# DLRM tower with two CIN layers: moments tiled by class, contraction at each chunk's end, dense layers per chunk

## What is computed

```python
e = stack([tbl_f[ids[:, f]] for f in range(32)], axis=1)        # (512, 32, 64)
x1 = einsum('oc,bcd->bod', W0, outer(e, e)) + b0                # outer: (512, 32*32, 64)
x2 = einsum('oc,bcd->bod', W1, outer(e, x1)) + b1               # outer: (512, 32*128, 64)
z = concatenate([x1.sum(2), x2.sum(2)], axis=1)                 # (512, 256)
h = relu(concatenate([z, dense_ctx], 1) @ W_top1 + b_top1)      # (512, 512)
y = relu(h @ W_top2 + b_top2) @ W_top3                          # (512, 1)
```

## Time and profile before

| | |
|---|---|
| median of 3 runs | 286.87 us |
| the profiled execution, its own time | 285.69 us |
| its span, first to last instruction | 283.9 us |
| TensorE busy (matmul records) | 244.8 us |
| TensorE loading weights | 177.0 us |
| ScalarE busy | 162.9 us |
| GpSimd busy (all but 0.6 of it gathers) | 143.2 us |
| VectorE busy | 132.7 us |

### The profile page before, as it was taken

How to read it: one execution, slowest core, us unless ns; L and a number is a source line. 1 busy time by engine, 2 the same in 40 slices (tenths; PEclk the granted TensorE clock), 3 DMA queues, 4 the chain that set the end, 5 groups by cost and what they waited for, 6 DMA issues and landing times.

```text
span 283.9 us, 6021 instructions
## 1 busy us (share of the span) xinstructions
PE 244.8 (86%) x2356; PEld 177.0 (62%) x2356; DVE 132.7 (47%) x350; ACT 162.9 (57%) x471; POOL 143.2 (50%) x134
## 2 busy tenths in 40 slices
PE   0699981149778997999999999999999999999985
PEld 0588870125545545777768777879777779995331
DVE  0100399355778928865607765626766620000111
ACT  0488883035566996669875668886566664001100
POOL 5777789777777777777777777700000000000000
PEclk9999998557999999999999999999999999999999
DMA  4911100011111112421111431100230000351000
GB/s 138 346 37 25 30 15 9 19 24 30 23 23 29 22 29 61 110 58 20 30 25 24 122 79 22 29 7 0 60 95 0 2 2 0 93 161 52 0 0 0
DMA packets 10366, 13.14 MB, mean 46 GB/s; under 512 B 4161, under 2 KB 5313, under 8 KB 10338
## 3 DMA queue, kind: packets, MB, share of 16 engines
q1 hardware_dynamic: 5058, 8.23, 9.7%
q0 software_dynamic: 4096, 4.20, 7.7%
q10 hardware_dynamic: 1184, 0.32, 0.6%
HBM read 8.54 MB, written 0.00 MB: 30 GB/s over the span
## 4 chain that ended last, share of the span: by engine, by line
PE 59%; POOL 26%; issue 10%; DMA 3%; DVE 1%; SPq 0%; ACT 0%; POOLq 0%
POOL XG L231 26%; PE psum L530 18%; PE psum L458 11%; PE psum L507 9%; PE psum L518 6%; PE psum L548 3%; PE psum L592 3%; PE psum L535 3%; DMA main<-in_w1t 3%; PE psum L486 2%; PE psum L586 2%; PE psum L588 1%; PE psum L520 1%; PE psum L587 1%; DMA XG<-in_tbl,idx 1%
## 5 line engine op out<-in xcount | busy, mean ns | idle before, releaser
L231 POOL DMA_INDIRECT XG<-in_tbl,idx x128 | 142.6, 1114 | 40.9 <-issue 38.1
L349 ACT ACTIVATE main<-psum 128x256 f32<-128x256 f32 (+5 forms) x324 | 104.7, 372 | 38.1 <-PE psum L520 16.5
L311 DVE TENSOR_TENSOR PP<-main 128x512 f32<-128x512 f32 x128 | 82.8, 689 | 31.4 <-PE psum L507 31.3
L530 PEld LDWEIGHTS psum<-main,DT 128*128 128x128 f32 x512 | 64.4, 191 | 24.9 <-issue 24.4
L530 PE MATMUL psum<-main,DT 128*128 128x128 f32 x512 | 77.4, 285 | 0.0
L349 ACT ACTIVATE U<-psum 128x512 f32<-128x512 f32 (+1 forms) x129 | 49.6, 436 | 31.5 <-PE psum L507 25.4
L507 PE MATMUL psum<-PP,main 64*32 64x320 f32 x1024 | 50.2, 450 | 4.9 <-DVE PP L317 4.9
L518 PE MATMUL psum<-ident,U 128*128 128x128 f32 x256 | 38.8, 274 | 1.2 <-ACT U L349 0.9
L518 PEld LDWEIGHTS psum<-ident,U 128*128 128x128 f32 x256 | 29.6, 141 | 6.9 <-issue 3.9
L486 PE MATMUL psum<-ident,XG 128*128 128x128 f32 x128 | 20.8, 291 | 14.4 <-DMA XG<-in_tbl,idx 12.4
L275 DVE TENSOR_TENSOR main<-main 128x240 f32<-128x240 f32 (+15 forms) x62 | 18.9, 382 | 17.3 <-ACT main L349 17.3
(11 more groups left out here) (45 smaller groups left out, 114.4 us busy)
## 6 DMA issues: line engine op xcount, KB each, us to landing
main<-in_w1t SPq DMA_DIRECT2D x4, 512.0 KB, 8.8
XG<-in_tbl,idx POOLq DMA_INDIRECT x128, 2.7
GL<-main SPq DMA_DIRECT2D x32, 64.0 KB
GG<-main SPq DMA_DIRECT2D x32, 64.0 KB
main<-in_wt SPq DMA_DIRECT2D x2, 512.0 KB, 4.1
W0Z<-in_w0z SPq DMA_DIRECT2D x1, 512.0 KB, 11.2
GG<-in_near_a ACTq DMA_DIRECT2D x1, 136.0 KB, 2.4
GG<-in_near_b ACTq DMA_DIRECT2D x1, 136.0 KB, 2.7
```

Of the source, the lines that this page charges most:

```text
L231: pool.indirect_dma_start(out=XG[:, f, :], out_offset=None, in_=tables[f], in_offset=bass.IndirectOffsetOnAxis(ap=idx[:, c, f:f + 1], axis=0),
L311: v.tensor_tensor(pp[:, :, g * P:(g + 1) * P].rearrange("p b (s j) -> p b s j", s=NS), in_main(at, [[2 * XW, KB], [0, NS], [1, HF]]), in_m ...
L349: return a.activation(dst, src, ACT.Copy)
L530: mm(z, DT[:, m, t, :], T[:, (c + 1) % 2, t].rearrange("p (h m) b -> p h m b", h=2)[:, :, m, :], start=m == 0 and t == 0, stop=False)
```

## The change

- The moments are tiled by class: the 256 near pairs, the small class and x itself form 16 blocks of 20 columns, 320 in all, cut into four classes of 80. Class q goes into the array's column tile q, for each sample: a step has 32 matmuls of 80 columns, into the same two banks. ScalarE copies 640 elements per partition straight into U, which holds a whole chunk; `turn`, T, T2 and the DMAs on SP go away.
- Products are made for 8 samples per half at a time (j counts them, 8 per chunk, two steps each) with two buffers PP. The columns with x itself are written by ScalarE (`e_columns`).
- The contraction of a chunk (8 + 69 matmuls of 128 columns) stands after its last step, all in one piece, with the x groups 4 to 7 of the next chunk in it, after 8, 28, 51 and 77 matmuls. Groups 0 to 3 stand behind j = 0, 2, 4 and 6.
- The dense layers of chunk c run with 128 columns inside chunk c+1, those of the last chunk at the end. Their weights are loaded at the start.
- The coefficient matmuls come in another order (near and cross by halves of the fields), nine of the 18 coefficient groups are transposed ahead of x group 7 of chunk 0, the others two per j in chunk 0, copied by ScalarE.
- A gather of chunk c, fields f to f+7, waits for NG*c + f//4 - 2 transposed groups. In chunk 0 gathers from field 12 on wait for coefficient matmuls.

The diff, cut to its core:

```diff
+NBK = 2 * NS
+BW = HF + 4
+NP = NBK * BW
+NQ = 4
+CW = NP // NQ
+TB = HF + 1
+NT = NBK // NQ * TB
+NN = NT + 1
 BP = P // 2
 KB = 4
 NK = BP // KB
-CL = 2 * P
-CX = CL + F
-NP = CX + F
+NJ = NK // 2
+KP = 2 * KB
 XW = HF + NS
-PPS = 3
+PPS = 2
 F1, F2 = 512, 256
 DC = 16
-NQ = 4
 NG = 8
-XK = 7
-NDT = F // 2 + 2
+NDT = (NN + 3) // 4
+NE = 9
+VORDER = [*[("near", m) for m in range(HF)], *[("cross", m) for m in range(HF, F)],
+          *[("near", m) for m in range(HF, F)], *[("cross", m) for m in range(HF)]]
+
+XPAIR = {0: 0, 2: 1, 4: 2, 6: 3}
+TURN = ((8, 4), (20, 5), (23, 6), (26, 7))
...
+def coefficient_groups(j):
+
+    return range(NE + 2 * j, min(NE + 2 * j + 2, NDT))
...
+    uses = [("x", 0, g) for g in range(NG - 1)] + [("d", 0, n) for n in range(NE)] + [("x", 0, NG - 1)]
...
-            by = pair_dve if use[0] == "d" and use[2] % 3 != 1 else pair_act
+            by = pair_dve if use[0] == "d" and use[2] % 2 and use[2] < NE else pair_act
...
             sp.dma_start(idx[:, :, :], ids).then_inc(ids_in, 16)
-            sp.dma_start(CROSS, cross_a).then_inc(cross_in, 16)
-            sp.dma_start(CROSS_B, cross_b).then_inc(cross_in, 16)
             for i in range(4):
                 sp.dma_start(W1T[:, 8 * i:8 * i + 8, :], w1t[:, 8 * i:8 * i + 8, :]).then_inc(w1_in[i], 16)
+                if i == 1:
+                    sp.dma_start(CROSS, cross_a).then_inc(cross_in, 16)
+                    sp.dma_start(CROSS_B, cross_b).then_inc(cross_in, 16)
             sp.dma_start(W0Z[:, :, :], w0z).then_inc(w0z_in, 16)
-            for c in range(NC):
-                sp.wait_ge(b7_ev, use7["t2", c, NK - 1] + 1)
-                if c:
-                    sp.wait_ge(z0_mm, c)
-                else:
-                    sp.wait_ge(dt_mm, NDT)
-                for q in range(4):
-                    for h in range(2):
-                        for dst, r in ((GL, 0), (GG, F)):
-                            sp.dma_start(
-                                dst[32 * q:32 * q + 32, h, :, :],
-                                T2[64 * h + r:64 * h + r + F, c % 2, 8 * q:8 * q + 8, :],
-                            ).then_inc(g_in, 16)
-                if c == NC - 1:
-
-                    sp.dma_start(WT1, wt1[0:2 * P, :].rearrange("(k p) n -> p k n", p=P)).then_inc(mlp_in, 16)
-                    sp.dma_start(WT1C, wt1[2 * P:, :]).then_inc(mlp_in, 16)
-                    sp.dma_start(WT2, wt2.rearrange("(k p) n -> p k n", p=P)).then_inc(mlp_in, 16)
+            sp.dma_start(WT1[:, :, :], wt1[0:2 * P, :].rearrange("(k p) n -> p k n", p=P)).then_inc(mlp_in, 16)
+            sp.dma_start(WT1C[:, :], wt1[2 * P:, :]).then_inc(mlp_in, 16)
+            sp.dma_start(WT2[:, :, :], wt2.rearrange("(k p) n -> p k n", p=P)).then_inc(mlp_in, 16)
...
                 for f in range(F):
                     if c and f % 8 == 0:
                         pool.wait_ge(gathered[f // 8], 128 * c)
-                    if c and f % 4 == 0:
-                        pool.wait_ge(x_mm, NG * (c - 1) + f // 4 + 1)
+                    if c == 0 and f % 4 == 0 and f >= 12:
+                        pool.wait_ge(v_mm, 2 * (f - 8))
+                    if c and f % 8 == 0:
+                        pool.wait_ge(x_mm, NG * c + f // 4 - 2)
...
+            dve.wait_ge(v_ev, F)
+            for _ in moves(1):
+                pass
+            wrap_field(0)
+            dve.wait_ge(v_ev, 2 * F)
+            for _ in moves(0):
+                pass
+            for n in range(NE):
+                coefficients_out(n)
...
-            def products(c, k):
-
-                n = NK * c + k
+            def products(c, j):
+
+                n = NJ * c + j
                 if n >= PPS:
-                    dve.wait_ge(t_mm, n - PPS + 1)
-                pp = PP[:, n % PPS]
-                x0 = (c % 2) * xt_n + KB * k * 2 * XW + NS
+                    dve.wait_ge(t_mm, 2 * (n - PPS + 1))
+                pp = PP[:, n % PPS].rearrange("p b (s w) -> p b s w", w=BW)
+                x0 = (c % 2) * xt_n + KP * j * 2 * XW + NS
                 for g in range(2):
                     at = x0 + g * HF
-                    v.tensor_tensor(pp[:, :, g * P:(g + 1) * P].rearrange("p b (s j) -> p b s j", s=NS),
-                                    in_main(at, [[2 * XW, KB], [0, NS], [1, HF]]),
-                                    in_main(at, [[2 * XW, KB], [2 * g - 1, NS], [1, HF]]), ALU.mult)
-                x = XT[:, c % 2, KB * k:KB * k + KB, NS:NS + F]
-                v.tensor_copy(pp[:, :, CX:NP], x)
-                x = x.rearrange("p b (g m) -> p b g m", g=2)
-                v.tensor_tensor(pp[:, :, CL:CL + 2 * NS].rearrange("p b (g m) -> p b g m", g=2),
+                    v.tensor_tensor(pp[:, :, g * NS:(g + 1) * NS, 0:HF],
+                                    in_main(at, [[2 * XW, KP], [0, NS], [1, HF]]),
+                                    in_main(at, [[2 * XW, KP], [2 * g - 1, NS], [1, HF]]), ALU.mult)
+                x = XT[:, c % 2, KP * j:KP * j + KP, NS:NS + F].rearrange("p b (g m) -> p b g m", g=2)
+                v.tensor_tensor(pp[:, :, :, HF].rearrange("p b (g m) -> p b g m", g=2),
                                 x[:, :, :, 0:NS], x[:, :, :, NS:HF], ALU.mult).then_inc(pp_ready, 1)
 
-            repeat(0)
-            products(0, 0)
             for c in range(NC):
-                for k in range(1, NK):
-                    products(c, k)
-                    if c == 0:
-                        for n in range(3 * k - 3, min(3 * k, NDT)):
-                            if pair_out["d", 0, n][0] is pair_dve:
-                                dve.wait_ge(dt_mm, n + 1)
-                                v.tensor_copy(coefficient_slot(n), bank[pair_bank["d", 0, n]]).then_inc(pair_dve, 1)
-                    if k == XK + NG - 2 and c < NC - 1:
+                repeat(c)
+                for j in range(NJ):
+                    products(c, j)
+                    if j == NJ - 3 and c < NC - 1:
...
+            def e_columns(n):
+
+
+                c, j = divmod(n, NJ)
+                act.wait_ge(*pair_out["x", c, NG - 1])
+                if n >= PPS:
+                    act.wait_ge(t_mm, 2 * (n - PPS + 1))
+                copy(PP[:, n % PPS].rearrange("p b (s w) -> p b s w", w=BW)[:, :, :, HF + 1:HF + 3],
+                     XT[:, c % 2, KP * j:KP * j + KP, NS:NS + F].rearrange("p b (s w) -> p b s w", w=2)).then_inc(e_ready, 1)
+
+            for g in range(NG - 1):
                 x_out(0, g)
+            for n in range(NE):
+                dt_out(n)
+            x_out(0, NG - 1)
+            e_columns(0)
+            e_columns(1)
...
+            def moments_out(c, k):
+
+                n = NK * c + k
                 act.wait_ge(t_mm, n + 1)
-                if n >= 2:
-                    act.wait_ge(tr_mm, n - 1)
-                src = psum[:, 2 * (n % 2):2 * (n % 2) + 2, :]
-                copy(U[:, n % 2, :].rearrange("p (q n) -> p q n", q=2), src[:, :, 0:CL])
-                copy(U2[:, n % 2, :].rearrange("p (q n) -> p q n", q=2), src[:, :, CL:NP]).then_inc(u_ev, 1)
...
+                copy(U[:, c % 2, :, :, KB * k:KB * k + KB].rearrange("p n h i -> p h n i"),
+                     psum[:, 2 * (n % 2):2 * (n % 2) + 2, 0:KB * CW].rearrange("p h (i n) -> p h n i", i=KB)).then_inc(u_ev, 1)
...
+            for g in range(NG - 1):
                 x_group(0, g)
-            pe.wait_ge(left, 1)
-            pe.wait_ge(zeroed, 3)
+            for n in range(NE):
+                coefficients(n)
+            x_group(0, NG - 1)
...
             def moments(c, k):
 
                 n = NK * c + k
-                pe.wait_ge(pp_ready, n + 1)
+                if k % 2 == 0:
+                    pe.wait_ge(pp_ready, n // 2 + 1)
+                    pe.wait_ge(e_ready, n // 2 + 1)
                 if n == 0:
                     pe.wait_ge(v_ev, 2 * F)
                 if n >= 2:
                     pe.wait_ge(u_ev, n - 1)
                 for i in range(KB):
-                    for h in range(2):
-                        lo = BP * h
-                        last = mm(bank[2 * (n % 2) + h][F * i:F * i + F, 0:NP],
-                                  XT[lo:lo + BP, c % 2, KB * k + i, NS:NS + F], PP[lo:lo + BP, n % PPS, i, :], start=True, stop=True)
+                    for q in range(NQ):
+                        for h in range(2):
+                            lo = BP * h
+                            last = mm(bank[2 * (n % 2) + h][F * q:F * q + F, i * CW:i * CW + CW],
+                                      XT[lo:lo + BP, c % 2, KB * k + i, NS:NS + F],
+                                      PP[lo:lo + BP, n // 2 % PPS, k % 2 * KB + i, q * CW:q * CW + CW], start=True, stop=True)
                 last.then_inc(t_mm, 1)
...
-            def turn(c, k):
-
-                n = NK * c + k
-                pe.wait_ge(u_ev, n + 1)
-                use = ("t", c, k)
-                pe.wait_ge(*pair_out[pair_before[use]])
-                for i in range(4):
```

(102 more changed lines are left out.)

353 lines of the change are left out of this document (169 added, 184 removed).

## The result

The changed kernel takes 300.3 us, median of four runs (297.6 to 306.2), and the kernel before 286.9 us on the same chip: ratio 1.043, 95% interval 1.034 to 1.053. It is slower. The forecast was 278, faster; the time lies in the range and the sign is wrong. The profiled execution is the longest of the four, 306.23 us with a span of 304.4 (the others have 295.8 to 299.0), and TensorE stood at half clock for 27 us of its last chunk, so part of that chunk's time belongs to this execution alone.

A forecast was written before the change was run, and what follows sets the result against it. Serial gather batches were to bound it, 52.3 us per chunk against 44.5 for TensorE and VectorE: T(3) 222.1 plus last chunk 51.3 ends at 273.4, clock 2.5 makes 275.9, plus 1.8 gives 277.7, forecast 278; range 262 to 303.

The forecast's parts named there:

- The step that failed: Moment phase: VectorE's products set the pace, 2.6 us per 8 samples, eight such per chunk 20.8 us.
- The moment step: TensorE's 64 passes of 80 columns per step: 0.75 us, between 0.70 (only columns count) and 2.8 (price per pass).
- rivals with other mechanisms: Slower cases: passes with a price that doesn't shrink (308 us, chance 0.20) and clock staying down (291 us, chance 0.13).
- the start: Chunk 0: additions starve the gathers, last landing at 54 us, T(0) = 64.6, moments begin at 69.3.
- My first rival: Moment phase: each pass has a price that doesn't shrink with width; 1.75 us per step, time 308 us, chance 0.20.
- the five starts of the earlier trace: Evidence for cheap moment passes: five start within 40 ns on different tiles of the array, before the change.
- the gather loop: Serial gather batches waiting for x groups: 11.9 + 14.6 + 13.8 + 12.0 = 52.3 us per chunk, over the 44.5 otherwise.
- under 2.6: ScalarE's copies per 8 samples stay under VectorE's 2.6 us, except about 3.5 in the first chunk.
- the small product: VectorE's product of 128 elements per 8 samples: 0.29 us.
- the turn's idle time: Between a chunk's contraction and the next moments: 2.1 us plus first product 2.6, TensorE idle 4.7 us per chunk.
- The end: Last chunk's dense layers: 44 passes 4.8 us, with copies, hand-overs and output 8.6 us, where 25.3 stand now.
- The clock: Half clock after idle times adds 2.5 us; as a rival, the clock stays down: 291 us, chance 0.13.

The follow-up runs named there:

- the eighths: Kernel before, each of its 16 moment passes per step issued as eight of 40 columns, consecutive passes on different tiles: 392.4 us, ratio 1.370.
- quarters: Kernel before, each moment pass issued as four of 80 columns, consecutive on one tile: 530.8 us (kernel before 399.1 there); by turns over tiles, elsewhere: 297.4 us.

## Why the prediction was wrong, point by point

**The step that failed** is the moment phase, "8 samples take 2 x 1.14 + 0.3 = 2.6 us" as VectorE's pace, "Eight such per chunk are 20.8 us", with nothing charged for the program's length. The moment step itself was right: 0.75 us forecast, 1.58 for two measured, and in groups of eight the starts are 7 ns apart. But a pair of steps is 256 instructions, and at the 13.0 to 14.3 ns of the eighths that is 3.3 to 3.7 us, over the 2.6. With the layers and x groups between them a chunk's moment phase has some 2200 instructions, 29 to 31 us of supply for the 19.8 that I priced; 31 to 34 were measured in the first three phases, 27 to 33 with gates and h1 order mended, 21 to 24 (22.2 in the mean) with half the passes as well. The halving is the test: 29.6 us, against 4 x (29 to 31 - 22.2), 27 to 35, by this sum. With half the passes and nothing else the kernel takes 284.0 us against the forecast's 278, so some 17 of the 22 us go with this step, part of which may be the array's own saving.

That 300.3 us lies inside the range is luck. The range reached up to 303 for rivals with other mechanisms, and the start gained 9 us that I had not forecast.

My first rival had the size: per step 1.75 us, time 308, and it named the fact that speaks for it, 128 instructions in a row. But I gave it the mechanism of a price per pass in the array, then discounted it to 0.20 with the five starts of the earlier trace rows. Those answer only how fast the array takes passes that are there. The supply was to be read before: 19 packets on q8 for 2356 passes, and two of them in 22 us of the steady steps.

**Two stated rules.** In the trace the 256 instructions of two steps go out in 1.58 us when nothing disturbs them, the loads of blocks start no less than 3.4 us apart, and the stops stand at the ends of blocks. The Trainium skill, Runtime: NRT & Kernel Launch, section "Instruction fetch mechanics", says that programs come in 16 KiB blocks of 256 instructions, which agrees with the q8 rows, and that this is hidden because instructions are dispatched more slowly than blocks arrive. For TensorE the trace disagrees: 6 ns per instruction out, 13 in. The Trainium skill, TensorE: Matmul & The Clock Gate, section "Wait — 56ns, not 53.3ns?", says that starts come no closer than about 25 ns. By it two steps would take 3.2 us; 1.58 were measured, so for passes on different tiles it does not hold.

**Gathers.** The gates act as described: gathers wait 42.4 us for x groups, and a batch beside VectorE starts at 174.95 and the next at 191.72, 16.8 us for the forecast's 14.6; the next follows 16.7 us later, for 13.8. They were longer because group 1 and group 3 themselves stood behind stopped moments. But the gather loop was no longer the sole bound: without the gates the kernel is at most 2.9 us faster. TensorE waited for gather DMAs four times, at most 2.3 us, not nine times 2 to 5. With half the passes alone the forecast's picture is there: nine waits, 0.6 to 5.6 us long, and chunks of 56 us for its 52.5. So the term was real, and the supply stood in front of it. The changed kernel, then that run (groups on the page):

```profile
L493 PE MATMUL psum<-ident,XG 128*128 128x128 f32 x128 | 21.0, 292 | 8.9 <-DMA XG<-in_tbl,idx 7.2
```

```profile
L493 PE MATMUL psum<-ident,XG 128*128 128x128 f32 x128 | 22.3, 305 | 26.3 <-DMA XG<-in_tbl,idx 25.0
```

**A wait that I missed.** ScalarE's h1 copy at j = 1 needs TensorE's layer 1 of j = 2, and two moment copies stand behind it (190.40). I counted ScalarE's time ("under 2.6") and not its order. Alone at most 3.6 us, with the gates 12.6.

**Start.** Additions took 6.85 us per half for the forecast's 9.6 (280 ns each for 382; those of 240 elements 404 for 572), and the second half did not starve the gathers, which took 0.94 us each beside it (43.91). So the last gather of chunk 0 ended at 44.9 us and had landed before 46.4, not at 54, and moments began at 60.3, not 69.3. This 9 us gain hid as much of the loss. What makes the additions shorter and lets the gathers through was not tried; the half beside the coefficient matmuls took as long (6.77 us) as the one behind them.

**Single prices.** The 1024-element product was right (1222 ns for 1.22 us), two of them 2.36 for 2.28; the small product was 415 ns for 290; the 640-element copy 0.71 us as forecast; the turn's idle time 4.42 for 4.7. The last copy, the contraction and the turn together took 26.3 us, 1.6 more than the forecast's 1.0 + 17.2 + 1.8 + 4.7. The end: from the last contraction's end (274.74 + 15.57) to 304.4 are 14.1 us where "8.6" stood; the passes there ran at half clock (3.78 us for the 16 of layer 2, which took about 2.05 in the chunks before).

**The clock** is the other part that I undersized: 2.5 us. The profile shows half clock behind each turn and in some pieces between, 72 us in all in this execution and 58 in another, where the kernel before had 20.5. Two steps take 2.44 us behind the turn for 1.58. It doesn't come from the stops: halving the passes left it at 58 us, and at 38 once gates and h1 order were mended, while the time fell by 17 and by 29.6 us. It fell with the waits of those two, and no run shows what it costs by itself; the four executions of the changed kernel go from 306.2 us at a mean granted clock of 0.88 to 297.6 at 0.94.

## What to carry to other kernels

Cutting matmuls into more and narrower ones costs instructions even where it costs no columns. Count TensorE's instructions (four per float32 matmul here) against the time of the stretch that they stand in, at some 13 to 14 ns each, and read the packets of the program's queue: here every phase that wanted a block in less than 3.3 to 3.7 us stopped at the ends of blocks. And where a new order makes an engine wait, read that engine's order for what stands behind; two such waits can each look free while the other stands.

## What was unexpected

- The program's supply: 256 instructions per 3.3 to 3.7 us, shown by the break that moves 14 records a step, and by stops that all stand a multiple of 256 instructions apart.
- A pass's price depends on where the one before went: 64 passes of 80 columns took 2.88 us with four in a row per tile, 0.92 to 1.14 us by turns over eight tiles, and 0.79 in the changed kernel (1.58 for two steps).
- Less work in the array lowered the granted clock: with 20 columns for 80 it averaged 0.76 to 0.78 over the span (0.88 to 0.94 in the changed kernel), and the time rose.
- One chip ran the kernel before in 399 us. Its quarters there had long waits while gathers ran and none afterwards. The cause stays open.
